# First weights of three stages loaded and split in four parts, and layer 0's context in four parts among its weights

## The reference

```
x = x + tanh(g_xattn[0]) * xattn0(layernorm(x), ctx)   # 16 query heads, 4 key/value heads of 96
x = x + tanh(g_ffn[0])   * ffn0(layernorm(x))          # a linear layer and 8 gated low-rank experts
x = x + tanh(g_xattn[1]) * xattn1(layernorm(x), ctx)   # 32 heads, 8 key/value heads of 128, normed q and k
x = x + tanh(g_ffn[1])   * ffn1(layernorm(x))          # mixing of 4 streams
```

## Time and profile before

| | us |
|---|---|
| median of 3 runs | 2596.14 (2595.49 to 2597.87) |
| the profiled execution: its time | 2597.39 |
| its span in the trace | 2595.6 |
| TensorE busy | 2386.6 (92%) |
| DVE busy | 1493.9 (58%) |
| ACT busy | 1078.5 (42%) |
| POOL busy | 1048.7 (40%) |
| mean granted TensorE clock | 0.954 |

### The profile page before, as it was taken

The page is one execution under the profiler, slowest core; times in us unless marked ns, Lnnn a source line. Parts: engine busy times, 40 slices in busy tenths (PEclk is TensorE's granted clock), DMA queues, the critical chain, the costliest instruction groups (busy, mean ns, idle before and its releaser), DMA issues. The chain is left out here.

```text
span 2595.6 us, 34684 instructions
## 1 busy us (share of the span) xinstructions
PE 2386.6 (92%) x12976; PEld 2201.3 (85%) x12976; DVE 1493.9 (58%) x2344; ACT 1078.5 (42%) x2448; POOL 1048.7 (40%) x844
## 2 busy tenths in 40 slices
PE   8999999979998899999889889999999999999714
PEld 6888888868998789999779779999999999999713
DVE  6222222123300567678667467888777777777797
ACT  3222222122311456667611155555555555554413
POOL 3000000000000356677554367777676766764110
PEclk9999999989999799999989999999999999999757
DMA  6222222143323222332133223333333333322001
GB/s 201 69 67 74 69 73 70 49 157 113 95 66 99 92 74 81 94 93 73 54 109 95 87 72 92 107 99 100 101 97 110 98 101 103 97 85 83 6 0 51
DMA packets 161241, 224.36 MB, mean 86 GB/s; under 512 B 31718, under 2 KB 124290, under 8 KB 160050
## 3 DMA queue, kind: packets, MB, share of 16 engines
q1 hardware_dynamic: 161074, 222.14, 27.7%
HBM read 183.81 MB, written 38.29 MB: 86 GB/s over the span
## 5 line engine op out<-in xcount | busy, mean ns | idle before, releaser
L1270 DVE TENSOR_TENSOR attend_w_lo<-attend_w_raw,attend_w_hi 128x1024 fp32r<-128x1024 f32 (+1 forms) x184 | 273.3, 1485 | 208.4 <-ACT attend_w_hi L1125 125.0
L1005 POOL TENSOR_TENSOR attend_w_hi<-attend_w_raw,attend_one 128x1024 fp32r<-128x1024 f32 (+1 forms) x178 | 332.7, 1869 | 126.6 <-DMA attend_w_raw<-in_wo 61.2
L1445 PE MATMUL attend_ps_gemm<-normed_hi,attend_w_hi 128*128 128x400 f32 x704 | 246.4, 350 | 21.8 <-DVE attend_w_lo L1270 21.8
L1141 ACT ACTIVATE attend_p<-attend_p,attend_neg_max 100x361 f32<-100x361 f32 x256 | 150.9, 591 | 260.7 <-DVE attend_neg_max L1309 260.7
L1445 PE MATMUL attend_ps_gemm<-attend_o_hi,attend_w_hi 128*128 128x400 f32 x704 | 250.6, 356 | 6.1 <-issue 4.4
L1445 PE MATMUL attend_ps_gemm<-normed_lo,attend_w_hi 128*128 128x400 f32 x704 | 244.9, 348 | 0.0
L1445 PE MATMUL attend_ps_gemm<-attend_o_hi,attend_w_lo 128*128 128x400 f32 x704 | 243.7, 346 | 0.0
L1445 PE MATMUL attend_ps_gemm<-normed_hi,attend_w_lo 128*128 128x400 f32 x704 | 243.6, 346 | 0.0
L1445 PE MATMUL attend_ps_gemm<-attend_o_lo,attend_w_hi 128*128 128x400 f32 x704 | 243.6, 346 | 0.0
L301 DVE TENSOR_TENSOR context_k_square<-context_k_rows 128x512 f32<-128x512 f32 (+1 forms) x46 | 31.8, 692 | 346.5 <-ACT context_k_rows L226 346.4
L1150 ACT ACTIVATE attend_p<-attend_p,attend_exp_inv 100x361 f32<-100x361 f32 (+1 forms) x384 | 207.8, 620 | 0.0
(11 more groups left out here) (302 smaller groups left out, 6405.6 us busy)
## 6 DMA issues: line engine op xcount, KB each, us to landing
attend_w_raw<-in_wq SPq DMA_DIRECT2D x88, 512.0 KB, 4.3
attend_w_raw<-in_wo SPq DMA_DIRECT2D x64, 512.0 KB, 4.3
middle_w_raw<-in_wf SPq DMA_DIRECT2D x26, 512.0 KB, 4.2
attend_w_raw<-in_wo SPq DMA_DIRECT2D x32, 384.0 KB, 3.8
context_ctx_raw<-in_ctxT SPq DMA_DIRECT2D x8, 1456.0 KB, 7.0
attend_k_raw<-scratch_k SPq DMA_DIRECT2D x64, 180.5 KB, 3.7
context_ctx_raw<-in_ctxF SPq DMA_DIRECT2D x22, 512.0 KB
scratch_v<-context_v_out SPq DMA_DIRECT2D x44, 256.0 KB, 2.1
```

The source lines that it names most:

```text
L1005: pool.tensor_tensor(hi, w_flat(w_raw, j % RAW, j), one[:hi.shape[0]].to_broadcast(hi.shape), ALU.mult).then_inc(w_hi_done, 1)
L1141: act.activation(p[:, slot, h], p[:, slot, h], ACT.Exp, bias=neg_max[:, slot, h:h + 1], accum_out=exp_sum[:, slot, h:h + 1]).then_inc(expe ...
L1270: dve.tensor_tensor(w_flat(w_lo, j % SPLIT, j), w_flat(w_raw, j % RAW, j), w_flat(w_hi, j % SPLIT, j).bitcast(F32), ALU.subtract).then_inc ...
L1445: mm = pe.matmul(out, left[a](c), right[b](c), start=(c == 0 and a == b == 0), stop=(c == chunks - 1 and a == 1))
```

## The change

In `project_layer0` a context is loaded, rounded and split in four parts of two chunks, each load with its own semaphore. The first part of context 0 goes ahead of all else; weights 0 and 1 follow, then the other three parts, then weights 2 to 15. The four parts of context 1 are issued behind weights 12, 13, 14 and 15, ahead of the tokens. ACT and DVE take each part of context 0 just before the two key tiles of its chunks. `mean(0)` moves from before the second batch to between that batch's key and value groups.

In `attend` and `middle` the first weight tile (j = 0) is loaded by four DMAs of 128 KB and split in four parts by ACT and DVE; TensorE's first product waits for each part when it comes to its chunks. In `attend` the gate (and mask) load is issued behind the first two tiles, ACT does tanh after rounding the first three tiles, and DVE waits for the gate only before its loop over the units. In `middle` ACT waits for POOL's constants after the parts of the first tile. The waits of the other tiles are renumbered.

```diff
 # project_layer0
-            context(0)
-            for i in range(NW):
+            context(0, 0)
+            weights(0)
+            weights(1)
+            for part in range(1, PARTS):
+                context(0, part)
+            for i in range(2, NW):
                 weights(i)
+                if i >= NW - PARTS:
+                    context(1, i - NW + PARTS)
             for s in range(2):
                 load_x(s)
-            context(1)
...
-            split_context(0)
-            for i in range(NW):
+            for part in range(PARTS):
+                round_context(0, part)
+                for i in range(part * PC, (part + 1) * PC):
+                    round_weights(i)
+            for i in range(NC, NW):
+                round_weights(i)
...
-                    pe.wait_ge(ctx_lo_done, c // PAIRS + 1)
+                    pe.wait_ge(ctx_lo_done, c // PC + 1)
...
-            mean(0)
             for b in range(1, B):
-                pe.wait_ge(ctx_lo_done, 2 * b + 2)
+                pe.wait_ge(ctx_lo_done, PARTS * (b + 1))
                 for kind in "kv":
+                    if kind == "v" and b == 1:
+                        mean(0)
 # attend
-            sp.dma_start(gate[:], io["gx"][layer]).then_inc(side_load, 16)
...
+                if j == 0:
+                    for part in range(PARTS):
+                        col = slice(part * PW, (part + 1) * PW)
+                        sp.dma_start(w_raw[:, 0, col], wq[0][:, col]).then_inc(part_load[part], 16)
+                    return
...
             for j in range(RAW):
                 tile(j)
+            sp.dma_start(gate[:], io["gx"][layer]).then_inc(side_load, 16)
...
+            for part in range(PARTS):
+                col = slice(part * PW, (part + 1) * PW)
+                act.wait_ge(part_load[part], 16)
+                act.activation(w_hi[:, 0, col], w_raw[:, 0, col], ACT.Copy).then_inc(part_hi_done, 1)
+            for j in range(1, SPLIT):
+                act.wait_ge(w_load[j % RAW], loads_of(j) * 16)
+                act.activation(w_flat(w_hi, j, j), w_flat(w_raw, j % RAW, j), ACT.Copy).then_inc(w_first_done, 1)
             act.wait_ge(side_load, 16 * (1 + layer))
             act.activation(gate[:], gate[:], ACT.Tanh).then_inc(gated, 1)
-            for j in range(SPLIT):
...
-            dve.wait_ge(gated, 1)
...
 # attend, product(); the same in middle
+                    if first and c * PARTS % chunks == 0:
+                        part = c * PARTS // chunks
+                        if part < PARTS - 1:
+                            pe.wait_ge(part_lo_done, part + 1)
+                        else:
+                            pe.wait_ge(w_lo_done, 1)
```

More of the change, by code:

```diff
@@ L424, in project_layer0 @@
         w_lo_done = sem("w_lo_done")
-        ctx_load = sem("ctx_load")
+        ctx_load = [sem(f"ctx_load{part}") for part in range(PARTS)]
         ctx_hi_done = sem("ctx_hi_done")
@@ L803, in attend @@
         w_first_done = sem("w_first_done")
+        part_load = [sem(f"part_load{part}") for part in range(PARTS)]
+        part_hi_done = sem("part_hi_done")
+        part_lo_done = sem("part_lo_done")
         w_hi_done = sem("w_hi_done")
@@ L910, in attend, with loads_of @@
         CONSTS = 14 if layer == 1 else 7
+        def loads_of(j):
+            return len([i for i in range(1, j + 1) if i % RAW == j % RAW])
         def norm_pair(a, k):
@@ L1680, in tile @@
             def tile(j):
+                if j == 0:
+                    first = io["wf"][0].rearrange("p (c n) -> p c n", c=NC)
+                    for part in range(PARTS):
+                        at = slice(part * PC, (part + 1) * PC)
+                        sp.dma_start(w_raw[:, 0, at], first[:, at]).then_inc(part_load[part], 16)
+                    return
                 if j >= RAW:
@@ L1775, in round_wh @@
                 act.activation(wh_hi[:], wh[:], ACT.Copy).then_inc(wh_hi_done, 1)
-            for j in range(EARLY):
+            for part in range(PARTS):
+                at = slice(part * PC, (part + 1) * PC)
+                act.wait_ge(part_load[part], 16)
+                act.activation(w_hi[:, 0, at], w_raw[:, 0, at], ACT.Copy).then_inc(part_hi_done, 1)
+            act.wait_ge(consts, CONSTS)
+            for j in range(1, EARLY):
                 act.wait_ge(w_load[j % RAW], 16)
@@ L1809, in split @@
                     return
+                if j == 0:
+                    for part in range(PARTS):
+                        at = slice(part * PC, (part + 1) * PC)
+                        dve.wait_ge(part_hi_done, part + 1)
+                        lo = dve.tensor_tensor(w_lo[:, 0, at], w_raw[:, 0, at], w_hi[:, 0, at].bitcast(F32), ALU.subtract)
+                        if part < PARTS - 1:
+                            lo.then_inc(part_lo_done, 1)
+                        else:
+                            lo.then_inc(w_lo_done, 1)
+                    return
                 if j < EARLY:
-                    dve.wait_ge(w_first_done, j + 1)
+                    dve.wait_ge(w_first_done, j)
                 else:
```

100 lines of the change are left out of this document (66 added, 34 removed).

## The result

The changed kernel takes 2589.66 us (median of 20 runs, 2582.83 to 2595.53) against 2596.24 for the kernel before on the same chip (20 runs, 2591.11 to 2601.46). The ratio is 0.9974 [0.9967, 0.9981], so 6.6 us faster. The forecast was 14.1 us, its range ended at 2588.5: the sign was right, the size was not. The profiled execution took 2584.8 us (span 2583.0), near the low end of its spread. So I compare stages, and wherever more traces exist I take them all. A stage is counted from POOL's first memset of it to that of the next.

The account below looks back on a forecast made before the run. In the changed stages TensorE sets the pace (busy 1769.60 of 1860.20 us). Terms 5.5 + 4.5 + 1.5 + 2.3 + 0.3 = 14.1 us, taken from 2596.1, gave 2582.0 us, range 2576 to 2588.5.

Parts of the forecast that it names:

- Start of `project_layer0`: Context 0 in parts: first matmul at about 545.9 instead of 551.4, 5.5 us earlier; bounds 0 to 6.9.
- wait before the second batch: Earlier context 1 in `project_layer0` removes the 2.77 us wait and the half clock behind it: 4.5 us; bounds 0 to 5.
- `attend` layer 0: First matmul 2.6 us earlier, TensorE's third product at 855.4 instead of 856.91: 1.5 us; bounds 0 to 2.6.
- `middle`: First matmul at 1312.3 instead of 1314.60: 2.3 us; later tiles' small delays ahead of TensorE's second product; bounds 1 to 4.
- `attend` layer 1: First matmul 3.5 us earlier, but POOL's chain of squares holds TensorE: 0.3 us; bounds 1 lost to 3.5 gained.
- Heads pass whole: Rival: POOL's chain and the query copies in `attend` don't hold TensorE, 1.1 and 3.2 us more: 2577.7; chance 0.12.
- weights starve: Rival in `project_layer0`: tiles 12 to 15 or context 1 come 4 us later, stall and half clock stay: 2586.5; chance 0.13.
- the parts landed apart: Its opposite was a rival: the four DMAs end together, heads stay, only context 1 gains: 2591.6; chance 0.08.
- Slower: Rival: transfers' fixed 2.65 us paid one after the other, later tiles in `middle` and `attend` late: 2600; chance 0.04.
- over 1 us apart: Sign of being wrong in the changed kernel's trace: parts of a load landing over 1 us apart.
- The fit that the prediction quotes: Skill's DMA time of 2.0 us plus size by 436 GB/s: four 128 KB parts 9.2 us without overlap, one tile 3.2.

Follow-up runs that it names:

- e3: Kernel before with only `project_layer0` as changed, `attend` and `middle` as before: 2588.44 us, ratio 0.9964.
- e12: Kernel before with only `project_layer0` changed, all its new loads but `mean(0)` still ahead of the second batch: 2587.67 us, ratio 0.9967.
- e11: Kernel before with only the opening of `project_layer0` in parts; context 1, in parts too, behind tokens and `mean(0)`: 2589.97 us, ratio 0.9976.
- e7: Changed kernel, tanh between second and third tile; in `middle` DVE adds the tokens' halves before the first tile's remainders, the rest behind: 2586.73 us.
- e6: Changed kernel with `mean(0)` in `middle` one product later, behind TensorE's third product: 2586.41 us, ratio 0.9959.
- e9: Changed kernel with keys and values loaded behind the third weight tile in both `attend` stages: 2582.96 us, ratio 0.9951.
- e4: Kernel before with only `attend` (both layers) and `middle` as changed, `project_layer0` as before: 2598.98 us, ratio 1.0008.
- e14: Changed kernel with keys and values behind the third tile (as e9) and `mean(0)` in `middle` one product later (as e6): 2584.58 us, ratio 0.9954.
- e13: Kernel before with only keys and values issued behind the third weight tile in both `attend` stages: 2596.59 us, ratio 1.0.
- e15: The kernel of e9 run again, beside the changed kernel: 2584.78 us, ratio 0.9955.
- e5: Changed kernel with tanh between the second and third tile in `attend`, not behind the third: 2586.29 us, ratio 0.9961.

## Why the prediction was wrong, and where it was right

- **Start of `project_layer0`, 5.5 us; wait before the second batch, 4.5 us.** Right in size and in mechanism: 10.4 us together by the stage's length (the totals of e3 and e12 are 8.6 us below the kernel beside them; the traces don't place the rest). The first part was on hand after 3.14 us (forecast 3.54), and no wait for weights appeared inside batch 0. The division was off: the early context 1 is worth 2 us, since the parts alone already save 1.15 us of the wait and the half clock behind it (e11). And there was luck in it: the forecast had context 1 rounded by 568.5 with 3 us to spare, but ACT took up the last weight tile only at 568.66 and ended the context at 572.34. The spare was gone, and a wait of 0.49 us was left, behind which the clock happened to stay at 1.00.
- **`attend` layer 0, 1.5 us.** Right, 1.5 us. Tanh stands behind the third tile, TensorE waits for the query remainders before its third product, and that product starts 15.3 us into the stage instead of 17.0. The table load takes 1.29 us up to its instruction, as forecast. The Trainium skill (ScalarE: Activation LUTs, What ACT_TABLE_LOAD costs) adds a drain of 1.38 us to the load; no trace here shows one.
- **`middle`, 2.3 us: this step failed.** The prediction put the second and third tile "0.4 to 0.5 us later than before (three more issues)" and DVE's sums 0.5 us later, "all ahead of TensorE's second product". Three more issues are 1.3 us by its own 0.43 us each. ACT took the third tile up 1.75 us later in the stage (8.05 us against 6.30; 7.5 to 9.0 in the seven traces of this form, 6.1 to 6.8 in the eight of the old), the sums began 10.5 us after the start instead of 8.8, and the last took 2.15 us instead of 0.58 beside a POOL that now rounds without a pause, so TensorE waited 2.59 us. The Trainium skill (GPSIMD Engine Reference, Key points) says that POOL's memory interfaces are shared with DVE, and that DVE instructions with two memory inputs contend for them; this sum is one, and the traces agree: in e7, where POOL does not work beside them, the last two sums took 0.98 and 0.57 us, beside POOL 2.57 and 2.15. Even without that wait the stage was not clearly shorter: e6 and e7 cure it, and the gain goes at a later tile. I had priced a head as if what it gives were kept to the end of the stage, in the one stage whose later limits I had not looked at. Measured: +0.8 us.
- **`attend` layer 1, 0.3 us: this step failed too.** The forecast had POOL's squares start "just as late" as before, and a longer wait of TensorE at the scores. The squares start at 15.2 to 16.9 us in six traces of this form, against 14.2 to 15.3 in five of the old one, and TensorE waits for them at the row sums ahead of its third product, where it did not wait at all; at the scores it waits 1.41 us instead of 1.77. For squares that start as before, with tanh and its table load (1.48 us) and the rounding (1.06) ahead of the copy at 1474.11, ACT would have to take up the third tile at 1471.6, 1.1 us sooner in the stage than before. Its load was issued 1.6 us sooner, but it was taken up 0.4 us later: the sum counted SP's issue times and took the time from issue to landing as it was, and this grew from 4.8 to 6.7 us behind keys and values. Measured: +2.0 us. e9 shows the cause of the late tile by removing it; how much of the growth is the queue reached sooner, and how much the slower packets, is not shown.
- **The rivals.** "Heads pass whole" was wrong for three of four heads, "weights starve" did not occur, and the parts landed apart. "Slower" priced a late second and third tile in `middle` and `attend` by paying the fixed cost in series. Its mechanism was wrong, as the parts of 128 KB landed after a median of 2.6 us each and overlapped, but its symptom was there: a third tile 1.75 us later in `middle` and 0.4 us later in layer 1. The last of the four parts also landed 1.5 us behind the third in `middle` and 1.3 in layer 1, which the prediction had named as a sign of being wrong ("over 1 us apart"). The fit that the prediction quotes beside this rival stands in another section of the page it names (the Trainium skill, DMA: Bandwidth & Descriptors, Anatomy of one DMA — SWDGE (gpsimd) path), and is for a DMA on the GpSimd path; here SP issues them all.
- By size: 14.1 forecast, some 9 by the stages, 6.6 measured. By the stages the two failed terms are 5.4 us (3.1 and 2.3) of the 7.5 missing. By the totals `project_layer0` gave 8.6 of 10.0 (e3, e12), and the three split first tiles cost 1.9 where 4.1 were to be gained (e4): 7.4 us, nearly all of it in these tiles. The two ways of counting differ by what a stage mean leaves open.

What stays open: e9's opening of layer 1 is 3.5 to 5.7 us ahead of the changed kernel's and its median 6 us lower, yet its stages in three traces (943.6, 944.1, and 943.0 in e14) are not clearly shorter than 944.6. Those three executions were 2.6 to 3.7 us above their medians. The traces go part of the way: in them TensorE stood at half clock for 27.3, 27.3 and 23.9 us of layer 1's stage, against 23.9 on average in the six of the changed form. Each us of it costs half a us; without that cost the stage takes 930.5 us against 932.6. So some 2 us of the gain stand in this stage, partly hidden by half clock. 100 us into the stage, by the same instruction, e9 is 1.0, 4.4 and 1.3 us ahead of the three traces of the changed kernel itself. The other 3 to 4 of the 6 us no trace places, and why the half clock differs from execution to execution was not tested.

## What to carry to other kernels

Here a head shortened by splitting its first load was kept only where the later inputs of the opening came forward as well: before splitting, read which loads stand between the first tile and the next ones, and put those that are needed last behind them. In layer 1 the order was worth nothing while the head was long (e13), and the parts nothing while the order was wrong (e4), so try them together. Count the issue time of the parts against the loads behind them. And read a stage past its opening: where a chain on another engine ends last 40 us later, an earlier start only lengthens a wait.

## What the runs showed of the hardware

- In layer 1's opening a part of 128 KB had landed after a median of 2.6 us and a load of 512 KB after 4.7, with issues about 0.5 us apart, so loads overlap well. A first tile in column blocks goes in packets of 1 KB, 55 to 59 ns each on average in the three openings of the changed trace (median 46), where whole rows of 4 KB took 180 to 204 ns (median 159): four of the small ones, 218 to 235 ns, hold an engine longer for the same bytes.
- A short idle time of TensorE does not always bring the half clock: behind 0.49 us in the changed kernel, 0.99 in e9, 1.38 in e15 and 1.62 in e11 the clock stayed at 1.00 (2.4 GHz); behind 2.36 us in e5 and 2.59 in `middle` it was at 0.76 over the next 7 us, and behind 2.91 in layer 1 at 0.80, so partly at 1.2 GHz.
- The same DVE sum of 128 x 400 took 0.58 us beside an idle POOL and 2.15 us beside a working one; the sum of 128 x 800 took 0.98 and 2.57 us.
